# Self-attention of a decoder layer: projection parts spread one to a step, shifts through the maxima's PSUM banks

## The reference, cut to what matters

```python
# x: (2, 2048, 512), 16 heads of D = 32
def _L0_attn_ref(x, qkv_w, qkv_b, proj_w, proj_b):
    scale = (c // H) ** (-0.5)
    qkv = (x @ qkv_w + qkv_b).reshape(b, n, 3, H, D)
    q, k, v = jnp.moveaxis(qkv, 2, 0)
    attn = jnp.einsum('bnhd,bmhd->bhnm', q, k) * scale
    attn = jax.nn.softmax(attn, axis=-1)
    out = jnp.einsum('bhnm,bmhd->bnhd', attn, v).reshape(b, n, c)
    return out @ proj_w + proj_b          # this last product is in the next stage
...
x = _layernorm(x + _L0_attn_ref(x, ...))
```

## Time and profile before

| | |
|---|---|
| median of 3 runs | 4436.65 us (4436.28 to 4440.53) |
| the profiled execution | 4429.49 us |
| its span, first to last instruction | 4427.9 us |
| mean granted TensorE clock | 0.936 |
| TensorE busy | 3804.4 us, 86% |
| VectorE busy | 2618.8 us, 59% |
| GpSimd busy | 2124.8 us, 48% |
| ScalarE busy | 1676.0 us, 38% |

### The profile page before, as it was taken

The page is one execution under the profiler, slowest core; times in us unless marked ns, Lnnn a source line. Parts: engine busy times, 40 slices in busy tenths (PEclk is TensorE's granted clock), DMA queues, the critical chain, the costliest instruction groups (busy, mean ns, idle before and its releaser), DMA issues. The chain is left out here.

```text
span 4427.9 us, 65605 instructions
## 1 busy us (share of the span) xinstructions
PE 3804.4 (86%) x17994; PEld 2244.2 (51%) x17995; DVE 2618.8 (59%) x4369; ACT 1676.0 (38%) x2902; POOL 2124.8 (48%) x1051
## 2 busy tenths in 40 slices
PE   4899999999999999999999678888819889888870
PEld 2444444444444544444444335454419778877760
DVE  3767766667676676666666455555414544445456
ACT  0155555555555455554555211111103433333340
POOL 0188878788887788887888411121130000000004
PEclk9799999999999999999999888989859999999995
DMA  5322121221121212212122211010112333223234
GB/s 186 89 64 75 40 62 56 63 71 56 56 61 55 80 37 65 71 38 74 43 75 72 84 38 39 28 57 28 38 46 72 120 105 102 93 98 107 87 117 166
DMA packets 202124, 322.52 MB, mean 73 GB/s; under 512 B 26107, under 2 KB 75675, under 8 KB 201797
## 3 DMA queue, kind: packets, MB, share of 16 engines
q1 hardware_dynamic: 182181, 266.45, 19.3%
q0 software_dynamic: 11168, 35.20, 2.5%
q10 hardware_dynamic: 8448, 16.78, 1.0%
HBM read 216.31 MB, written 46.44 MB: 59 GB/s over the span
## 5 line engine op out<-in xcount | busy, mean ns | idle before, releaser
L461 DVE TENSOR_REDUCE sa_part_max<-sa_mx 128x1 f32<-128x512 f32 x2124 | 1345.8, 681 | 686.7 <-PE sa_mx L576 683.4
L425 ACT ACTIVATE sa_prob<-sa_sc 128x512 f32<-128x512 f32 x2048 | 1143.0, 595 | 998.4 <-PE sa_sc L667 937.7
L265 POOL TENSOR_TENSOR sa_quad_sum<-sa_quad_sum,sa_prob 128x1024 f32<-128x1024 f32 x512 | 1208.7, 2393 | 88.6 <-ACT sa_prob L425 88.6
L576 PE MATMUL sa_mx<-sa_k_stack,sa_q_stack 96*128 96x512 f32 x2124 | 1012.4, 482 | 44.8 <-DVE sa_part_max L461 31.5
L667 PE MATMUL sa_sc<-sa_q_stack,sa_k_stack 98*128 98x512 f32 x2048 | 863.8, 422 | 30.6 <-ACT sa_prob L425 2.9
L265 POOL TENSOR_TENSOR sa_quad_sum<-sa_prob 128x1024 f32<-128x1024 f32 x256 | 618.9, 2433 | 453.2 <-ACT sa_prob L425 452.1
L576 PEld LDWEIGHTS sa_mx<-sa_k_stack,sa_q_stack 96*128 96x128 f32 x2124 | 409.2, 193 | 624.0 <-DVE sa_part_max L461 363.0
L1509 PE MATMUL ex_h<-ex_xT,ex_w 128*128 128x384 f32 (+2 forms) x2688 | 468.4, 330 | 113.8 <-issue 67.8
L590 PE MATMUL sa_pv<-sa_prob,sa_v 128*32 128x512 f32 x4104 | 554.9, 613 | 0.8 <-ACT sa_prob L425 0.8
L667 PEld LDWEIGHTS sa_sc<-sa_q_stack,sa_k_stack 98*128 98x128 f32 x2048 | 390.6, 191 | 308.7 <-ACT sa_prob L425 254.6
L1509 PEld LDWEIGHTS ex_h<-ex_xT,ex_w 128*128 128x128 f32 x2688 | 449.7, 195 | 141.0 <-issue 122.2
(11 more groups left out here) (178 smaller groups left out, 3431.1 us busy)
## 6 DMA issues: line engine op xcount, KB each, us to landing
sa_xT<-xT SPq DMA_DIRECT2D x70, 1024.0 KB, 5.4
ex_w_in<-in_L_ffn_w_dram SPq DMA_DIRECT2D x130, 512.0 KB, 4.1
sa_k_stack<-sa_hilo SPq DMA_DIRECT2D x432, 64.0 KB, 2.0
sa_q_stack<-sa_hilo SPq DMA_DIRECT2D x408, 64.0 KB, 2.0
eo<-ex_out POOLq DMA_DIRECT2D x8, 1536.0 KB, 7.4
ca_aT<-attnT SPq DMA_DIRECT2D x9, 1024.0 KB, 6.8
ca_xb<-in_x_dram SPq DMA_DIRECT2D x9, 1024.0 KB, 9.0
attnT<-sa_recip SPq DMA_DIRECT2D x33, 256.0 KB, 2.8
```

The source lines that it names most:

```text
L265: pool.tensor_tensor(quad_sum[:, i % 2, heads, :], so_far, prob[:, k, heads, :], ALU.add).then_inc(quad_ready, 1)
L425: act.activation(prob[:, kt % 4, j, :], sc[n % 2][:, :], ACT.Exp, scale=SCALE).then_inc(prob_ready, 1)
L461: dve.reduce_max(part_max[:, q, j, k:k + 1], mxp[bank % 3][:, :], AX_X).then_inc(max_read, 1)
L576: pe.matmul(mxp[bank % 3][:, :], q_stack[0:QK, j, at:at + P], k_stack[0:QK, buf, j, k * BANK:(k + 1) * BANK], start=True, stop=True).then_ ...
```

## The change

The 12 ops of a unit are kept, but each chunk now has three, and the four parts of an op go to four steps, at the end of the step behind the fourth score: steps 0, 1, 2, 4, or 5, 6, 8, 9, or 10, 12, 13, 14. The row sums move by one step (lag 7) to steps 3, 7, 11, 15, so that every step has one extra item. An op leaves misc in steps 5, 10 and 15. The shift's transposes no longer go through misc, which holds an unfinished op then, but take a turn in the round of the three maxima's banks, and are copied out in step 13 itself. ROUND lists the order in which the banks are used. Order of the ops and of the x loads changes with it; the reciprocals move to steps 4 and 5.

```diff
-    Op = namedtuple("Op", "what n ahead c kt load")
-    OPS = [Op("q", 2, 0, 0, 2, 0), Op("k", 0, 1, 0, 5, 1), Op("v", 0, 1, 0, 8, 1),
-           Op("q", 3, 0, 1, 2, 2), Op("k", 1, 1, 1, 5, 3), Op("v", 1, 1, 1, 8, 3), Op("k", 2, 1, 1, 11, 4),
-           Op("v", 2, 1, 2, 2, 4), Op("k", 3, 1, 2, 4, 5), Op("q", 0, 1, 2, 7, 6), Op("v", 3, 1, 2, 10, 5),
-           Op("q", 1, 1, 3, 2, 7)]
-    LOADS = [(2, 0), (0, 1), (3, 0), (1, 1), (2, 1), (3, 1), (0, 1), (1, 1)]
+    Op = namedtuple("Op", "what n ahead c load")
+    OPS = [Op("q", 2, 0, 0, 0), Op("k", 0, 1, 0, 1), Op("k", 1, 1, 0, 2),
+           Op("q", 3, 0, 1, 3), Op("k", 2, 1, 1, 4), Op("v", 2, 1, 1, 4),
+           Op("k", 3, 1, 2, 5), Op("q", 0, 1, 2, 6), Op("v", 3, 1, 2, 5),
+           Op("v", 0, 1, 3, 6), Op("q", 1, 1, 3, 7), Op("v", 1, 1, 3, 7)]
+    PARTS_AT = ((0, 1, 2, 4), (5, 6, 8, 9), (10, 12, 13, 14))
+    LOADS = [(2, 0), (0, 1), (1, 1), (3, 0), (2, 1), (3, 1), (0, 1), (1, 1)]
-    OP_AT = {(o.c, o.kt): i for i, o in enumerate(OPS)}
+    PART_AT = {(o.c, kt): (i, part) for i, o in enumerate(OPS) for part, kt in enumerate(PARTS_AT[i % 3])}
+    LEAVE_AT = {(o.c, PARTS_AT[i % 3][-1] + 1): i for i, o in enumerate(OPS)}
...
-    DEN_LAG = 6
-    SUMS_AT, DENS_AT, DIVIDE_AT, STORE_AT = 0, 2, (1, 0), 10
-    INVERT_AT = ((3, 1), (3, 3), (4, 1), (4, 3))
+    DEN_LAG = 7
+    SUMS_AT, DENS_AT, DIVIDE_AT, STORE_AT = 0, 3, (1, 1), 10
+    INVERT_AT = ((4, 1), (4, 3), (5, 1), (5, 3))
+    ROUND = []
+    for c in range(NQ):
+        for kt in range(T):
+            for i in range(HG):
+                ROUND.append(("max", (c * T + kt) * HG + i))
+                if (kt, i) == (T - EARLY, 2):
+                    ROUND.append(("shift", c))
@@ SyncE, for each kt (shift_rows stays behind this loop)
-                            if (c, kt) not in OP_AT:
+                            if (c, kt) not in LEAVE_AT:
                                 continue
-                            o = OP_AT[c, kt]
+                            o = LEAVE_AT[c, kt]
...
-                            if (op.what, op.n) == ("v", 3):
+                            if o == len(OPS) - 1:
                                 sp.wait_ge(v_ready, at(NQ) + 2 * NQ)
                                 load_wkv(sp.snap((u + 2) % G))
@@ VectorE
-                                reduce_max(at(NQ * NMAX) + (c + 1) * NMAX + m, m % NMAX, c * NMAX + m - LEAD)
-                                if i == 0 and kt == T - EARLY + 1:
-                                    leave_shift(at(NQ) + c + 1, at(NQ * 16 * HG) + (c + 1) * 16 * HG)
-                                if i == 1 and (c, kt - 1) in OP_AT:
-                                    leave(OP_AT[c, kt - 1])
+                                reduce_max(at(NQ * NMAX) + (c + 1) * NMAX + m, m % NMAX, ROUND.index(("max", c * NMAX + m - LEAD)))
+                                if (kt, i) == (T - EARLY, 2):
+                                    leave_shift(mxp[ROUND.index(("shift", c)) % 3], at(NQ) + c + 1, at(NQ * 16 * HG) + (c + 1) * 16 * HG)
+                                if i == 1 and (c, kt) in LEAVE_AT:
+                                    leave(LEAVE_AT[c, kt])
@@ TensorE
+                    def read(use):
+                        if use < 3:
+                            return max_read, at(NQ * NMAX) + NMAX + LEAD
+                        what, i = ROUND[use - 3]
+                        if what == "shift":
+                            return shiftT_ready, at(NQ) + i + 2
+                        return max_read, at(NQ * NMAX) + NMAX + LEAD + i + 1
...
-                        if before.c != op.c or o == 0:
-                            free = (shiftT_ready, at(NQ) + op.c + 1)
+                        if o == 0:
+                            free = (v_ready, at(NQ) + NQ)
...
-                                max_pass(at(NQ * NMAX) + (c + 1) * NMAX + m, m % NMAX, c * NMAX + m - LEAD, chunk % NQ, p if chunk < NQ else 1 - p)
+                                use = ROUND.index(("max", c * NMAX + m - LEAD))
+                                max_pass(m % NMAX, use, chunk % NQ, p if chunk < NQ else 1 - p, read(use))
                                 score(c, kt, i)
-                                if (c, kt) in OP_AT:
-                                    project_part(OP_AT[c, kt], i)
                                 if i == 1:
                                     burst(c, kt)
                                 if i == 2 and kt == T - EARLY:
-                                    transpose_shift(at(NQ) + c + 1)
+                                    use = ROUND.index(("shift", c))
+                                    transpose_shift(mxp[use % 3], at(NQ) + c + 1, read(use))
+                            if (c, kt) in PART_AT:
+                                project_part(*PART_AT[c, kt])
```

More of the change, by code:

```diff
@@ L456, in leave_psum, with reduce_max @@
                                          in1=hilo[:, i % 2, 0, :].bitcast(F32), op0=ALU.add, op1=ALU.subtract).then_inc(hilo_ready, 1)
-            def reduce_max(n, m, bank):
+            def reduce_max(n, m, use):
                 dve.wait_ge(max_mm, n + 1)
                 q, j, k = m // (HG * KQ), m // KQ % HG, m % KQ
-                dve.reduce_max(part_max[:, q, j, k:k + 1], mxp[bank % 3][:, :], AX_X).then_inc(max_read, 1)
+                dve.reduce_max(part_max[:, q, j, k:k + 1], mxp[use % 3][:, :], AX_X).then_inc(max_read, 1)
             def make_shift(reads, n):
@@ L473, in make_shift, with leave_shift @@
                                          in1=shift[:, :, :, 0].bitcast(F32), op0=ALU.mult, op1=ALU.subtract).then_inc(shift_ready, 1)
-            def leave_shift(n, ins):
+            def leave_shift(bank, n, ins):
                 dve.wait_ge(shift_mm, n + 1)
                 dve.wait_ge(shift_in, ins)
-                dve.tensor_copy(shiftT[:, :], misc[0:2 * HG, :]).then_inc(shiftT_ready, 1)
+                dve.tensor_copy(shiftT[:, :], bank[0:2 * HG, :]).then_inc(shiftT_ready, 1)
             split, n = 0, 0
@@ L496, in _ @@
             make_shift(NMAX, 0)
-            leave_shift(0, 0)
+            leave_shift(misc, 0, 0)
             for m in range(LEAD):
@@ L566, in project, with max_pass, transpose_shift @@
                     last.then_inc(proj_mm, 1)
[L568 to L573, removed]
+            def max_pass(m, use, c, buf, free):
+                if free is not None:
+                    pe.wait_ge(*free)
                 q, j, k = m // (HG * KQ), m // KQ % HG, m % KQ
                 at = c * BANK + q * P
-                pe.matmul(mxp[bank % 3][:, :], q_stack[0:QK, j, at:at + P], k_stack[0:QK, buf, j, k * BANK:(k + 1) * BANK],
+                pe.matmul(mxp[use % 3][:, :], q_stack[0:QK, j, at:at + P], k_stack[0:QK, buf, j, k * BANK:(k + 1) * BANK],
                           start=True, stop=True).then_inc(max_mm, 1)
-            def transpose_shift(n):
+            def transpose_shift(bank, n, free):
                 pe.wait_ge(shift_ready, n + 1)
+                if free is not None:
+                    pe.wait_ge(*free)
                 for q in range(TQ):
-                    last = pe.transpose(misc[0:2 * HG, q * P:(q + 1) * P],
+                    last = pe.transpose(bank[0:2 * HG, q * P:(q + 1) * P],
                                         shift[:, q, :, :].bitcast(F32).rearrange("p j a -> p (j a)"), ident[:, :])
@@ L606, in _ @@
                     for m in range(chunk, NMAX, KQ):
-                        max_pass(n, m, n, 0, 0, first=True)
+                        max_pass(m, n, 0, 0, (max_read, n - 2) if n >= 3 else None)
                         n += 1
@@ L617, in _ @@
             pe.wait_ge(const_ready, CONSTS)
-            transpose_shift(0)
+            transpose_shift(misc, 0, None)
             pe.wait_ge(stacked["q", 1], 16 * MOVES)
             for m in range(LEAD):
-                max_pass(NMAX + m, m, NMAX + m, 1, 0)
+                max_pass(m, NMAX + m, 1, 0, (max_read, NMAX + m - 2))
             for j in range(HG):
```

## The result

The changed kernel takes 4489.62 us, median of 4 runs (4479.21 to 4493.06), beside 4436.47 for the kernel before (4 runs, 4436.19 to 4440.53): ratio 1.0114, 95% interval 1.0096 to 1.0131. It is slower, by 53 us. The forecast was 4445 with a range up to 4482, so the time lies 8 us above the range. Of the forecast's three ways the time could go, the one with the largest chance came out (over 4445.5 us, 0.45); the size did not.

What follows compares the result with a forecast made beforehand. TensorE paces projection steps, TensorE and ScalarE in turn the others. Units 2119 plus stalls and clock 87 + 35 + 10 + 35 give 2286 us against 2278.3, so 4445 on the median; 8-in-10 range 4416 to 4482.

Steps and rivals of the forecast that it cites:

- The part step, 3.95: Attention-loop step with one projection part at its end: 3.95 us from first score to first score, summed from measured pieces.
- Unit of 264.9: One of the loop's eight units without stalls at chunk turns: 258.1 + 1.7 + 3.6 + 1.5 = 264.9 us.
- misc handed on, 0.40 and 0.65: Steps 5 and 10: TensorE waits for VectorE to empty misc, 0.40 us in four places, 0.65 in three, 3.6 a unit.
- Shift transposes, 0.43: Between third and fourth score, the shift's transposes add 0.43 us four times a unit, 1.7 us.
- Chunk 0 to 1: Shift rows queue behind 12 transfers of k1's stack; first score to maximum 14.86 us, stall 10.9, eight times 87 us.
- rival (c): The shift's first half meets GpSimd's adds in every chunk and stalls, some 4.8 us each: 154 more, 4599 us, chance 0.05.
- Rival (d): A part alone costs 0.83 us as four did, making the step 4.27: 123 more, 4568 us, chance 0.05.
- chunks 1 to 2, 2 to 3: Only an x load stands ahead of the shift rows; 4.6 us to the maximum, stall 0.65, sixteen times 10 us.
- chunk 3 to the next unit: Shift rows queue behind v1's leave and the wkv and vb loads: 9.0 us, stall 5.05, seven times 35 us.
- clock and restart: Behind the 15 long stalls TensorE's clock stays at 0.5, costing 2.3 us each: 35 us, bounds 0 and 77.
- the loop's own turn, 3.3 us, lies inside it three times: At three unit ends the loop's 3.3 us turn is hidden within the stall and adds nothing.
- Rival (b): SyncE's queue costs more: late transfers or clock at 0.5 for 10.2 us, 15 x 2.8 = 42 more, 4487 us, chance 0.13.

Runs made afterwards that it cites:

- Experiment 10: Experiment 5 with the reciprocals moved off the step of the leave, to (3, 3), (4, 1), (6, 1), (6, 3): 4418.71 us, ratio 0.9962.
- Experiment 2: The changed kernel with SyncE issuing the shift rows at step 14, ahead of step 15's transfers, in chunk 0 only: 4379.08 us, ratio 0.9866.
- experiment 3: The changed kernel with the shift rows issued in step 15 just ahead of the x load, in chunks 1 and 2 only: 4423.79 us, ratio 0.9975.
- Experiments 6 and 8: 6: experiment 1 with VectorE taking misc out behind its first maximum, not its second, 4272.55 us; 8: 6 with q1 projected before v0 in chunk 3, 4276.84 us.
- experiment 9: Experiment 6 with the third and fourth reciprocals moved from step 5 to step 6: 4255.04 us, ratio 0.9592.
- experiment 4: The changed kernel with the shift rows issued at step 14, ahead of step 15's loads, in chunk 3 only: 4452.17 us, ratio 1.0039.
- experiment 1: The changed kernel with SyncE issuing every chunk's shift rows at step 14, ahead of all that step 15 puts on the queue: 4284.17 us, ratio 0.9657.
- experiment 5: Experiment 1 with an op's four parts back in one step (2, 8 or 14), one behind each score: 4489.96 us, ratio 1.0111.

## Why the forecast was right in its mechanism and wrong in its size

**Right.**
- *The part step, 3.95.* Measured 3.91 to 3.94.
- *Unit of 264.9.* All that is not a turn's stall sums to 2335.6 - 221.9 = 2113.7 us for eight units, against 2119. Steps 1 to 14 alone are 1851 us. So the gain from spreading was real. Experiment 10 puts it at 102 to 135 us with the waits that come with it; the forecast had 120 less 29 for handing misc on, so about 90. Against the kernel before, all that is not a stall at a turn got 165 us shorter (2278.3 - 2113.7), where the forecast had 159; what makes up the part beyond spreading was not taken apart.
- *misc handed on, 0.40 and 0.65.* Step 10 is 4.38 to 4.41 and step 5 is 4.56, over 3.94: some 0.45, and 0.62. *Shift transposes, 0.43:* step 13 of chunk 0 is 4.37, also 0.43.
- *Chunk 0 to 1.* First score to next maximum was put at 14.86; the mean of eight is 14.73. Experiment 2 shows that the issue order is its cause.
- *L470.* 0.175 us in all chunks, with a margin of 0.51 to 0.61 us; rival (c) is out. Rival (d) is out with the part step.

**Wrong.** The stalls at the turns were to cost 87 + 35 + 10 + 35 = 167 us. Over a natural step 15 of 4.27 and step 0 of 3.94 they cost 221.9, 55 more; less the 5 that the units came out better, that is the 50 by which the loop is longer than forecast. In the forecast's own terms:

| term | forecast, us | measured, us | why |
|---|---|---|---|
| chunk 0 to 1 | 87 | 86 | |
| chunks 1 to 2, 2 to 3 | 10 | 32 | 5.98 from first score to maximum, not 4.6 |
| chunk 3 to the next unit | 35 | 47 | 9.4 at four turns (forecast 9.0), 12.5 at three |
| clock and restart | 35 | 56 | 32 at the 15 long stalls, 24 at the short ones |

The measured 56 is what is left of 221.9 when the other three are taken off, kind of turn by kind of turn. Two terms hold nearly all that is missing: 22 us of late landing and 24 us of clock, both at the sixteen short turns.

- *The step that failed first* is "0.31 + 0.38 + 0.15 + 2.48 + 1.28 = 4.6". The 1.28 from the last shift issue to TensorE was taken from the earlier trace rows, where nothing large stood ahead of the shift. Behind a megabyte of x it is 2.8 in the mean, and experiment 3, which changes only their order, brings 1.25 back.
- *The step that failed second* is the clock, charged to "the 15 long stalls" alone. Its price at those was about right, 32 us for 35. But the clock also fell behind eleven of the sixteen short stalls, of 1.87 us at the shortest shown (the window at 348.35). With a price of 0.65 they looked harmless; at about 2 us two in three of them dropped the clock. The kernel before had shown such a fall, behind the 2.15 us in which TensorE waits in the earlier trace rows; window of TensorE behind it, columns us, PE busy, clock, DMA share, GB/s:

```profile
1327.40:1330.80 3.40, 3.40 (x14) 0.50 0.00 0
```

  Together the sixteen short turns cost 56 us by the trace and 66 by the medians of experiment 3, where the forecast had 10 for them. This one kind of turn makes up nearly all of the 50.
- *The third* is "the loop's own turn, 3.3 us, lies inside it three times". It did not quite. TensorE's and SyncE's timelines at one such turn:

```profile
772.28 0.39 PE L688 MATMUL sa_sc<-sa_q_stack,sa_k_stack 98*128 98x512 f32 x1
...
785.58 0.79 PE L586 MATMUL sa_mx<-sa_k_stack,sa_q_stack 96*128 96x512 f32 x1 [9.44 <-DMA sa_q_stack<-sa_shiftT]
```
```profile
774.61 2.24 SPq L310 DMA_DIRECT2D sa_wkv<-in_L_attn_qkv_w_dram  x4
777.10 3.19 SPq L311 DMA_DIRECT2D sa_vb<-in_L_attn_qkv_b_dram  x1
780.44 2.73 SPq L331 DMA_DIRECT2D sa_q_stack<-sa_shiftT  x4
```

The one issue of vb took 3.19 us here, and 1.20 and 2.35 at the other two turns of the loop, where it is 0.35 at the turns of a unit inside it. From the last shift issue to TensorE it is 2.4 to 2.9 us at these three, and 1.25 at the others. Why either is longer is open; no run was made for it.

Rival (b) had named the right direction, "the queue costs more", and gave 4487, 3 us from the time. But it put the price on 15 turns at 2.8 each, by a clock that stays at 0.5 for 10.2 us, while most of the missing time (46 of 55 us) lies at the sixteen turns that it left alone. Its sum is right by luck and not by its mechanism.

Two later expectations failed in one way. Experiments 6 and 8 took a wait out of one step and found it in step 6. The forecast had named VectorE's load at step 5 as the reason for its 0.65; what it did not follow was what comes behind it on the same engine, and experiment 9 shows that the reciprocals of step 5 were what step 6 waited for.

## What to carry to other kernels

When work is moved to a later step, write down all that its queue then issues ahead of what the next stage waits for: here one call, moved one step up, turned 1.1% slower into 3.4% faster. Take the landing time of a transfer from a place with the same traffic ahead of it, since a megabyte ahead took it here from 1.25 to 2.8 us. Price a short stall with the clock behind it, and look for a wait that is taken off one step in the next one, while the late engine still has work queued.

## What the runs showed of the hardware that was not expected

- The granted clock went to the 1.2 GHz level (0.50 to 0.53) behind idle stretches of TensorE of 10.60 us and of 1.87 us alike; mean over the loop 0.95, and 1.00 with the stalls gone. Behind the sixteen stalls of 1.8 to 2.4 us it fell eleven times in the changed kernel, eight times in experiment 2 and twelve in experiment 4, so such a stall can be priced only in the mean.
- Four small transfers landed, as far as TensorE saw it, 1.24 us after their last issue with nothing large ahead, and 2.4 to 3.0 us with a 1 MB load ahead on the same queue.
- At the three turns of the loop TensorE waited 5.4 to 5.5 us for issue in experiment 1, with nothing late in the profile, where it stood idle for 2.9 to 3.3 in the kernel before. What makes the difference is open.
- L470, which takes 0.175 us where no GpSimd add is under way, waits as long as adds follow one another without a pause: 3.9 to 4.05 us in chunk 3 of the kernel before (the rest of one add and the whole of the next), about 1.0 in its chunk 0 and 0.82 to 0.92 in all 32 chunks of experiment 5 (the rest of the last add before a pause). In every case it ends 0.03 to 0.04 us after an add behind which GpSimd pauses for 0.29 us or more. That it is the pause that lets it in is read off these places and was not tried by a run.
